# Attention scores as float32r products of two heads at once, and a chunk's four scores ahead of its four maxima

## The reference

```python
w = jnp.einsum('bhnqd,bhnkd->bhnqk', fq, fk) * scale + fmask    # strided keys and the block's own
w = jax.nn.softmax(w, axis=-1)
```

```python
scores = jnp.einsum('bhqd,bhkd->bhqk', Q, K) / math.sqrt(Dh)
scores = jnp.where(causal, scores, jnp.finfo(scores.dtype).min)
attn = jax.nn.softmax(scores, axis=-1)
y = jnp.einsum('bhqk,bhkd->bhqd', attn, V)
```

## Time and profile before

| | us |
|---|---|
| median of 3 runs | 5484.69 (5483.14 to 5489.94) |
| the profiled execution | 5488.33, of which the span is 5486.5 |
| PE busy | 4990.8 (91% of the span) |
| DVE busy | 4167.8 (76%) |
| ACT busy | 2924.5 (53%) |
| POOL busy | 341.4 (6%) |
| embed, until about | 245 |
| sparse attention, until about | 976 |
| middle stage, until about | 1366 |
| dense attention, until about | 4729 |

### The profile page before, as it was taken

How to read it: one execution, slowest core, us unless ns; L and a number is a source line. 1 busy time by engine, 2 the same in 40 slices (tenths; PEclk the granted TensorE clock), 3 DMA queues, 4 the chain that set the end, 5 groups by cost and what they waited for, 6 DMA issues and landing times.

```text
span 5486.5 us, 80549 instructions
## 1 busy us (share of the span) xinstructions
PE 4990.8 (91%) x32000; PEld 2370.9 (43%) x32000; DVE 4167.8 (76%) x8394; ACT 2924.5 (53%) x3357; POOL 341.4 (6%) x308
## 2 busy tenths in 40 slices
PE   5378999665699999999999999999999999899999
PEld 4333444554233333433333333333333333488888
DVE  7566777576688888888888888888888877455555
ACT  3334555333255666666666666666666666432322
POOL 2210000355000000000000000000000000200000
PEclk8779999887799999999999999999999999899999
DMA  3554321354600120210210310200300000201010
GB/s 119 135 94 68 50 47 23 125 168 151 98 15 11 19 39 15 33 36 9 26 26 15 44 26 9 45 7 19 58 11 6 9 9 9 68 20 39 20 39 9
DMA packets 268673, 242.18 MB, mean 44 GB/s; under 512 B 73212, under 2 KB 247804, under 8 KB 264060
## 3 DMA queue, kind: packets, MB, share of 16 engines
q1 hardware_dynamic: 268296, 237.02, 19.5%
HBM read 143.49 MB, written 92.27 MB: 43 GB/s over the span
## 4 chain that ended last, share of the span: by engine, by line
PE 82%; DVE 9%; SPq 3%; ACT 2%; issue 2%; DMA 1%; POOL 0%; ACTq 0%; POOLq 0%; DVEq 0%
PE psum L756 21%; PE psum L718 19%; PE psum L692 17%; PE psum L73 12%; DVE maxes_dense L805 2%; PE psum L725 2%; PE psum L681 2%; SPq L607 2%; PE psum L721 1%; PE psum L695 1%; PE psum L704 1%; PE psum L1508 1%; SPq L593 1%; DMA keys_sparse<-parts_scratch 1%; PE psum L730 1%
## 5 line engine op out<-in xcount | busy, mean ns | idle before, releaser
L805 DVE TENSOR_REDUCE maxes_dense<-psum 128x1 f32<-128x512 f32 (+3 forms) x4608 | 2706.8, 640 | 508.6 <-PE psum L692 295.8
L776 ACT ACTIVATE probs_dense<-psum 128x1024 f32<-128x1024 f32 (+3 forms) x2304 | 2100.4, 951 | 1106.4 <-PE psum L718 819.8
L692 PE MATMUL psum<-keys_dense,queries_dense 96*128 96x512 bf16 (+3 forms) x4608 | 1693.8, 369 | 68.2 <-DMA queries_dense<-parts_scratch 55.6
L718 PE MATMUL psum<-queries_dense,keys_dense 99*128 99x512 bf16 (+3 forms) x4608 | 1669.6, 367 | 8.3 <-ACT probs_dense L776 7.2
L756 PE MATMUL psum<-probs_dense,values_dense 128*32 128x512 f32 (+3 forms) x9216 | 1133.4, 569 | 0.0
L718 PEld LDWEIGHTS psum<-queries_dense,keys_dense 99*128 99x128 bf16 x4608 | 447.5, 98 | 1164.4 <-ACT probs_dense L776 878.4
L692 PEld LDWEIGHTS psum<-keys_dense,queries_dense 96*128 96x128 bf16 x4608 | 451.6, 98 | 532.0 <-DVE maxes_dense L805 260.5
L795 DVE TENSOR_REDUCE maxes_sparse<-psum 128x1 f32<-128x144 f32 (+23 forms) x512 | 217.4, 425 | 189.5 <-PE psum L683 186.8
L1615 ACT ACTIVATE activated<-psum 128x512 f32<-128x512 f32 x208 | 124.6, 599 | 417.7 <-PE psum L73 406.3
L776 ACT ACTIVATE probs_sparse<-psum 128x1024 f32<-128x1024 f32 x224 | 226.7, 1024 | 217.0 <-PE psum L728 80.4
L756 PEld LDWEIGHTS psum<-probs_dense,values_dense 128*32 128x32 f32 x9216 | 187.9, 108 | 349.4 <-issue 300.3
(11 more groups left out here) (298 smaller groups left out, 5621.6 us busy)
## 6 DMA issues: line engine op xcount, KB each, us to landing
parts_scratch<-part SPq DMA_DIRECT2D x72, 512.0 KB, 4.1
v_scratch<-ve_s SPq DMA_DIRECT2D x96, 256.0 KB, 2.8
queries_dense<-parts_scratch SPq DMA_DIRECT2D x384, 64.0 KB
keys_dense<-parts_scratch SPq DMA_DIRECT2D x42, 512.0 KB, 16.9
keys_sparse<-parts_scratch SPq DMA_DIRECT2D x24, 512.0 KB, 18.9
queries_sparse<-parts_scratch SPq DMA_DIRECT2D x192, 64.0 KB
ao_scratch<-aos_dense SPq DMA_DIRECT2D x64, 128.0 KB, 2.0
ao_s<-ao_scratch SPq DMA_DIRECT2D x16, 512.0 KB, 4.6
```

Source lines behind the costliest of these rows:

```text
L692: m = pe.matmul(bank[:, 0:width], q[0:TROWS, h, b * P:(b + 1) * P], k[0:TROWS, h, kc * STRIP:kc * STRIP + width], start=True, stop=kc != j)
L718: m = pe.matmul(full[:, first_col:STRIP], k[:, h, c * P:(c + 1) * P], q[:, h, first_col:STRIP], start=True, stop=not diagonal)
L776: act.activation(probs[i % 6][:, :, first_col:STRIP], psum[:, at2:at2 + 2, first_col:STRIP], ACT.Exp, scale=SCALE, **extra).then_inc(exp_d ...
L805: m = dve.tensor_reduce(mx[:, h * BLOCKS + b, kc:kc + 1], bank[:, 0:width], AX.X, ALU.max)
```

## The change

Queries and keys are kept as two float32r parts (high and low), and three pairs of parts are summed instead of six: 48 rows, and two rows for minus the maximum, 50 together. Even heads lie on partitions 0 to 49, odd heads on 64 to 113, so that two heads stand on the two row halves of the array, and their matmuls are issued one behind the other. The part stores are two float32 tensors instead of three bf16 ones; the second ACT copy and the POOL subtraction go. Tiles of one chunk come in the order head 0, head 1 of the same query block, then the next block. The masks of the dense tiles and of the strided tiles leave TensorE: DVE adds them while it takes the maximum (`tensor_tensor_reduce`). The local tiles now hold two heads of one parity and two blocks. In `order`, all four scores of a chunk come first and then all four tiles. The hand of a unit is two transfers instead of one.

```diff
-TERMS = ((0, 0), (0, 1), (1, 0), (1, 1), (0, 2), (2, 0))
+TERMS = ((0, 0), (0, 1), (1, 0))
-MROWS = 3
+MROWS = 2
+SROWS = TROWS + MROWS
+HALF = P // 2
+PAIRS = GROUP // 2
...
-                for half in range(2):
-                    fs = slice(2 * half, 2 * half + 2)
-                    act.wait_ge(rested, 2 * s + half + 1)
-                    act.activation(p2[:, fs, :], rest[:, fs, :], ACT.Copy).then_inc(p2_set, 1)
...
-                    pool.tensor_tensor(p3[:, fs, :], rest[:, fs, :], p2[:, fs, :], ALU.subtract).then_inc(p3_set, 1)
...
-            return [(kc, h, b) for kc in range(j + 1) for h in range(GROUP) for b in range(BLOCKS)]
+            return [(kc, 2 * i + odd, b) for kc in range(j + 1) for i in range(PAIRS) for b in range(BLOCKS) for odd in range(2)]
...
-                    emit_tiles(4 * (m + lead(n)) + h + 1)
+                    if h == GROUP - 1:
+                        emit_tiles(4 * (m + lead(n)) + h + 1)
...
-            keys = [sbuf(st, f"keys_{stage}_{i}", [TROWS + MROWS, GROUP, TOKENS], BF16) for i in range(2)]
+            keys = [sbuf(st, f"keys_{stage}_{i}", [P, PAIRS, TOKENS], F32R) for i in range(2)]
...
                             width = (b + 1) * P if kc == j else STRIP
-                            m = pe.matmul(bank[:, 0:width], q[0:TROWS, h, b * P:(b + 1) * P],
-                                          k[0:TROWS, h, kc * STRIP:kc * STRIP + width], start=True, stop=kc != j)
-                            if kc == j:
-                                m = pe.matmul(bank[:, b * P:(b + 1) * P], ident_bf[:], tri_query[:], start=False, stop=True)
+                            m = pe.matmul(bank[:, 0:width], q[rows(h, TROWS), h // 2, b * P:(b + 1) * P],
+                                          k[rows(h, TROWS), h // 2, kc * STRIP:kc * STRIP + width], start=True, stop=True)
...
+                        if h % 2 == 0:
+                            continue
+                        pair = [psum[:, at2, :], psum[:, at2 + 1, :]]
...
-                            m = pe.matmul(full[:, first_col:STRIP], k[:, h, c * P:(c + 1) * P], q[:, h, first_col:STRIP],
-                                          start=True, stop=not diagonal)
+                            for odd, full in enumerate(pair):
+                                own = rows(odd, SROWS)
+                                m = pe.matmul(full[:, first_col:STRIP], k[own, h // 2, c * P:(c + 1) * P], q[own, h // 2, first_col:STRIP],
+                                              start=True, stop=not diagonal)
                             if diagonal:
-                                m = pe.matmul(full[:, first_col:first_col + P], ident_bf[:], tri_key[:], start=False, stop=True)
+                                m = add_masks([full[:, first_col:first_col + P] for full in pair], ident_bf, tri_key, False, True)
...
+                            if e >= 2:
+                                dve.wait_ge(side_freed, e - 1)
+                            m = dve.tensor_tensor_reduce(out=masked_scores[e % 2][:, 0:width], in0=bank[:, 0:width], in1=mask, scale=1.0, scalar=-3e38,
+                                                         op0=ALU.add, op1=ALU.max,
+                                                         accum_out=mx[:, h * BLOCKS + b, 0:1] if sparse else mx[:, h * BLOCKS + b, kc:kc + 1])
```

More of the change, by code:

```diff
@@ L575, in attend @@
             masks = []
+            masked_scores = [sbuf(st, f"masked_scores_{stage}_{i}", [P, STRIP]) for i in range(2)]
+            if not sparse:
+                causal_add = sbuf(st, "causal_add", [P, STRIP], BF16)
             if sparse:
-                str_keys = [sbuf(st, f"str_keys_{i}", [TROWS + MROWS, GROUP, NSTR], BF16) for i in range(2)]
+                after_add = sbuf(st, "after_add", [P, 2 * NSTR - P // STRIDE], F16)
+                str_keys = [sbuf(st, f"str_keys_{i}", [P, PAIRS, NSTR], F32R) for i in range(2)]
                 str_values = [sbuf(st, f"str_values_{i}", [P, NSTR // P, GROUP * GCOL]) for i in range(2)]
@@ L619, in attend_sp @@
                 for tile in keys:
-                    sp.dma_start(tile[TROWS:TROWS + MROWS, :, :], d["c_ones"]).then_inc(masks_in, 16)
+                    for odd in range(2):
+                        first_row = odd * HALF + TROWS
+                        sp.dma_start(tile[first_row:first_row + MROWS, :, :].bitcast(F32), ones_d).then_inc(masks_in, 16)
                 if sparse:
@@ L659, in attend_pe, with rows, add_masks @@
             def attend_pe():
-                pe.wait_ge(masks_in, 16 * (len(masks) + 2))
+                def rows(h, n):
+                    return slice(h % 2 * HALF, h % 2 * HALF + n)
+                def add_masks(banks, eye, mask, start, stop):
+                    for bank in banks:
+                        m = pe.matmul(bank, eye[:], mask[:], start=start, stop=stop)
+                    return m
+                pe.wait_ge(masks_in, 16 * (len(masks) + 4))
                 for kind, n, what in order:
@@ L681, in attend_pe @@
-                            pe.matmul(bank, q[0:TROWS, h, b * P:(b + 1) * P], str_keys[n // STRIPS % 2][0:TROWS, h, :],
-                                      start=True, stop=False)
-                            m = pe.matmul(bank[:, own:own + P // STRIDE], ident_h[:], mask_q[:], start=False, stop=True)
+                            m = pe.matmul(bank, q[rows(h, TROWS), h // 2, b * P:(b + 1) * P], str_keys[n // STRIPS % 2][rows(h, TROWS), h // 2, :],
+                                          start=True, stop=True)
@@ L684, in attend_pe @@
                         elif kc == "local":
-                            pe.matmul(bank, ident_h[:], tri0_q[:], start=True, stop=False)
-                            for h in range(GROUP):
-                                own = j * STRIP + b * P
-                                m = pe.matmul(bank[:, h * P:(h + 1) * P], q[0:TROWS, h, b * P:(b + 1) * P],
-                                              k[0:TROWS, h, own:own + P], start=False, stop=(h == GROUP - 1))
+                            add_masks([bank], ident_h, tri0_q, True, False)
@@ L690, in attend_pe @@
+                            for i in range(PAIRS):
+                                for block in (b, b + 1):
+                                    own, col = j * STRIP + block * P, (2 * i + block - b) * P
+                                    m = pe.matmul(bank[:, col:col + P], q[rows(h, TROWS), i, block * P:(block + 1) * P],
+                                                  k[rows(h, TROWS), i, own:own + P], start=False, stop=(i == PAIRS - 1 and block > b))
                         else:
                             width = (b + 1) * P if kc == j else STRIP
-                            m = pe.matmul(bank[:, 0:width], q[0:TROWS, h, b * P:(b + 1) * P],
-                                          k[0:TROWS, h, kc * STRIP:kc * STRIP + width], start=True, stop=kc != j)
```

236 lines of the change are left out of this document (118 added, 118 removed).

## The result

The changed kernel takes **6725 us** (median of four runs, 6657 to 6763) where the kernel before takes 5487 (four runs on the same chip, 5483 to 5493). The ratio, taken without the longest of the four (6762.92, span 6761.1, and the one that was profiled), is 1.221, 95% interval 1.212 to 1.231. The direction was forecast; the size was not: 5800 was predicted, and 6725 lies above the range's 6400.

The account below looks back on a forecast made before the run. TensorE's queue was taken as the bound, mostly in the dense stage; +281 dense, +74 sparse and -38 embed and middle gave +317, 5800 us. Forecast range 5540 to 6025; with serial halves and the nearest others 5430 to 6400.

Parts of the forecast that it names:

- The loop: Dense step: fourth tile waits for the first maximum, weighing and next scores behind it; 2.47 us without scores, 3.03 with.
- The halves work at once: Dense float32r scores: halves at once, a pair costing 0.22 to 0.23 us; serial halves rival, 6400 us, chance 0.13.
- DVE does not stay fed: Rival, dense step: DVE stays fed and paces at 2.48 to 2.54 us, 4955 us; chance wholly or in part 0.17.
- The refill: Float32r start after a wait adds 0.10 us, charged once a dense step, behind the fourth tile; upper end: twice, 3.13.
- Masks between pairs: Dense diagonal scores: masks stay between half-height pairs; +0.24 and 0.06 refill, 0.39 us over before, 256 steps, +100.
- the dense sum: Dense stage: +201 full steps, -58 diagonal tiles, +100 diagonal scores, +38 hand; together +281 us, ends +63 and +430.
- the step of the hand: Dense stage, each unit's hand: fourth tile waits for the second maximum, +0.62 us once in each of 64 units, +38.
- The clock: Rival: PE's idle 0.6 us a dense step lowers the granted clock in part; 6030 us and up, chance 0.02.
- my theory D: Expectation for added full-height matmuls: height in use over time sets the clock; eight: 6050 to 6350 us, two: 5400 to 5490.
- Sparse stage: Sparse stage: a unit goes from 18.4 us, without transfer waits, to 20.7, +2.3; +74 for 32, ends +32 and +128.
- Embed and middle: Shorter part preparation: ACT copies 11 us in embed, 20 in middle, POOL subtraction 7; together -38, at least -20.
- Tiles on the diagonal: Dense bursts with a diagonal tile: narrower first maxima shorten the wait; 0.35 less, 0.11 lost, 240 steps, -58 us.

Follow-up runs that it names:

- Three more orders: Kernel before, four scores before four tiles: 6034.42 us; changed kernel, two tiles after each pair: 5834.48; one after each pair, two after weighing: 5617.98.
- the kernel with the eight matmuls: Changed kernel with eight 128-row, 128-column matmuls ahead of every third tile of a dense burst, overwritten by it: 6209.47 us.
- the order alone: Kernel before, all products 96 or 99 rows high, with only a chunk's four scores issued ahead of its four tiles: 6034.42 us.
- the two: Changed kernel reordered (pair, tile, pair, tile, weighing, two tiles), diagonal masks gathered, two full-height matmuls ahead of every third dense tile and one per strided tile: 6117 us.
- before's own order: Kernel before, own order, with tile masks added by DVE with the maximum instead of by TensorE matmuls: 5421 us, ratio 0.988.
- run 230: Not a run number: "that run" is the changed kernel with eight full-height matmuls ahead of every third dense tile, 6209.47 us; 230 is microseconds.

## Why the prediction was right in direction and wrong in size

**The loop (right).** The largest term was that the fourth tile waits for the first maximum, and weighing and scores behind it. Three more orders were put through it before they ran: 3.34 was expected and 3.36 measured, 2.9 to 3.0 and 2.93, 2.5 to 2.75 and 2.70. The halves work at once, as chosen (3 ns between their starts), and DVE does not stay fed.

**The refill (mis-sized term).** I charged the 0.10 once, behind the fourth tile, and thought that the weighing hides the other. It is paid twice: fourth tile to weighing is 0.43 instead of 0.31, and scores to the first tile 0.57 instead of 0.46. The step is 3.17, not 3.03; 1116 of them make +357 instead of +201. My upper end of 3.13 had both. What holds the matmuls there was read from distances only, not tested.

**Masks between pairs (mis-sized term).** I took 0.30 us for the four masks, with 0.24 of it their columns. At the full clock, in the kernel with the eight matmuls, first score to first tile takes 1.30, 1.18, 1.07 and 0.95 at the four widths, 0.56 more on average than the 0.57 of a full step. 256 steps make +142 in place of +77.

With these two, the dense sum goes from +281 to 281 + 156 + 65 = 502; the run with the eight matmuls has 511. That they agree so well is partly luck. Some of the 511 is still clock; a burst that begins with a width of 128 saves 0.68 and not the 0.54 I had (3.17 to 2.49); and the step of the hand is 0.60 longer than a full one, as forecast, but in the kernel before it was 0.46 longer already (3.31 against 2.85), so +0.62 a unit was too much. These two make the sum smaller by some 50 us, an estimate, and what stands for them in the 511 is open.

**The clock (the step that failed).** The prediction held the dense stage at the full clock, and gave its loss 0.02, because "The gaps are short against PE's work around them". I looked at the gap alone, and by itself it does not decide: with a gap of 0.35 us in 3.36 and 99 rows, 1.00; with no gap and 51 rows one at a time, 0.51 to 0.66. The products' height never came up. With half-height pairs the gap does matter: 0.78 to 0.83 with PE idle for 113 to 124 us of 1000, 0.95 to 0.98 with 69 to 73. The Trainium skill (TensorE: Matmul & The Clock Gate, "A second HAM failure mode") tells of a kernel whose clock swung between the two levels as it paused briefly between groups of matmuls that cycled through banks. The kernel after does that; the order alone pauses in the same place and does not, so here the pause is not enough by itself. Part 1 of that page of the Trainium skill has the clock follow how busy the engine was of late; measured here, PE busy by the profile for 998 of 1000 us stood at 0.50 with 51 rows. Nor was my price right: I put a tenth of the steps at half speed and 225 us on it; it was 40% of the time and 532 us in the dense stage alone. Without this loss the time would have been inside the wide range (6209 against 6400) and still above the forecast's own 6025. What rule joins height, halves and idle time to the clock stays open: the balance of rows over time, my theory D, forecast the eight matmuls and failed on the two.

**Sparse stage (mis-sized).** +74 was predicted, its end was +128, and it is +245; with the filler in the dense stage only, +217. The order alone costs 67 there (711.0 against 643.7). The rest goes with masks between pairs, which are more frequent here, and with the clock: 0.76 over the stage against before's 0.94. How much each has was not separated.

**Embed and middle (mostly wrong).** -11 and 0 instead of -11 and -27. In embed the shorter preparation of parts is worth about what I said; that it meets it to 0.2 us is luck, since five runs whose embed is the same have their first sparse output at 314.8 to 324.5. In the middle stage nothing came of it, so what I took for a wait on ACT does not seem to be on the path. What holds that stage was not tested.

**Tiles on the diagonal (right in sign, a little small).** The term was worked out for the loop of the new order. There the trace of after has 2.49 and 2.99 for the two bursts where a full step has 3.17, 0.42 less on average and not 0.35, and before had 0.09 less and not 0.11: -0.34 a step in place of -0.24. Carried over to before's own order it gave 5410 to 5440, and 5421 was measured, but there no loop over the first maximum is shortened; the four masks leave PE's path, 0.23 a step. That the two sizes are alike is a coincidence. The wider instruction also runs at 0.61 to 0.62 a piece in a stream (603.62, 604.24, 604.85 in the sparse stage of after), faster than the 0.70 that I worked out from a 256-wide one.

The sum with the dense stage near the full clock is then 6209 - 5485 = +724, against the +317 predicted: by the marks of that run 230 too little in the dense stage, 143 in the sparse, 31 in embed, middle and the rest. The dense stage's clock adds 516 (6725 - 6209).

## What to carry to other kernels

Before products are cut to half the array's rows, ask what the array does at the same moment: here such products kept most of the clock only where a second one ran on the other half and PE had little idle time (0.94 to 0.98), and one at a time they took up to half the speed from everything in the stage, the full-height weighing too. When work is reordered around a small ring of banks, write down the loop through the first reuse of a bank; here it gave every step to 0.15 us. A useful part can hide in a losing change: run the parts singly.

## What the runs showed of the hardware that was not expected

- Same order, same instructions, 51 and 48 rows in place of 99 and 96: the dense stage's clock goes from 1.00 to 0.50, with PE busy for 998 of 1000 us. Being busy by the profile did not hold the clock.
- float32r pairs on both halves had a clock of 0.94 to 0.98 where PE was busy for 927 to 972 of 1000 us, 0.78 to 0.83 where for 876 to 887, and 0.99 to 1.00 when 128-row work stood in that gap. Products of 99 rows at 906 of 1000 had 1.00.
- A pair of heads on two halves costs as much as one: the halves start 3 ns apart, and four scores take 0.57 us to the first tile. But each change to a full-height matmul and back costs beyond its columns, some 0.3 us in all where one such change was saved: a pair to its masks takes 0.43 us, where the next pair would follow at 0.34 (3004.61 to 3004.95, with the refill), and two masks of 128 columns, 0.06 each in the kernel before, take 0.21.
- Eight full-height matmuls in a wait cost nothing in a full step and gave back 516 us; two behind the weighing, and one between overlapping half-height products, cost 558 together.
